# One transformer block with a mixture of experts: the tail of the kernel addressed by token numbers

## The chip, the core and the metric

The kernel runs on one core of one Trainium2 chip. The metric is device time in microseconds (us). Three runs of the kernel before gave 2922.35, 2927.16 and 2928.94 us, a median of 2927.16.

## What is computed

The reference is one adaptive-layernorm block over T = 2048 tokens of width C = 1024, all in float32:

```python
mod = (silu(c) @ wmod)            # six vectors of 1024: sa, ca, ga, sb, cb, gb
h = layernorm(x) * (1 + ca) + sa
x = x + ga * attention(h)         # 32 heads of 32, causal, plus 10 adapter keys, then @ w_proj.T
h = layernorm(x) * (1 + cb) + sb
logits = h @ gate_w               # 8 experts
topv, topi = top_k(logits, 2); w = softmax(topv)
x = x + gb * sum over the two chosen experts e of  w_e * (h @ expert_w[e])     # expert_w[e] is 1024 x 1024
```

Every token is sent to two experts of eight, so there are 4096 pairs of token and expert.

## The kernel before

Every large product is done as three fp32r products: the operands are split into a high half (rounded to fp32r) and a low half (what is left), and hi x hi, hi x lo and lo x hi are added up in PSUM. A split is a copy (the high half) and a subtraction (the low half). SBUF has 128 partitions (P), and C is 8 chunks (KC) of 128. The program is a row of stages; each has its own tiles and semaphores.

- **front** makes the modulation vectors, the layernorm, and q, k and v. In its last part (32 tiles of v, L634 to L641) ScalarE copies each finished PSUM tile out (L280) and the SP queue stores it. Meanwhile the GpSimd (POOL) queue writes zeros over the whole of `scratch_rows`, in 48 DMAs of 512 KB (L521), and in the middle of these it makes two low halves of weights (L488).
- **adapter_attention** and **attention** are not touched.
- **proj_out** (L1348) runs over 16 tiles of 128 tokens in a hardware loop. SP loads the 8 chunks of `w_proj`, then constants, then y and x of the tiles. TensorE waits for all 8 chunks and all constants before its first instruction. For tile n it transposes the normalized rows of tile n - 2 (`turn`, L1407), multiplies tile n (`project`, 48 matmuls at L670 to L672) and makes the 8 logits of tile n - 2 (`gate`, L1414: gate weights stationary, 128 tokens moving). In the first two rounds `turn` and `gate` work on zeros. VectorE scales and adds the residual (L1484, L1486), does the layernorm and hands over to GpSimd (L1516, L1518). x after attention goes to `scratch_x` in HBM, the normalized rows stay in SBUF (`h2`, 64 KB in each partition).
- **route** (L1521) starts when the last tile is done. It finds both experts of all 2048 tokens, the rank of each token within its expert, and from these the row of `scratch_rows` that each of the 4096 pairs gets: the experts' rows follow each other in blocks of 256 rows ("macros"), each expert rounded up to whole macros. Then GpSimd scatters the normalized rows there, 32 indirect DMAs of 512 KB (L1620), and waits until all have landed.
- **experts** (L1625) has an outer loop over the 8 experts and an inner one over the expert's macros; 18 macros in all with these inputs (36 halves of 128 rows, L1778 x36). Weights of the next expert are loaded and split by GpSimd (L1687, L1689) into a second buffer while TensorE works with the first. For each half TensorE turns 128 rows (L1713) and does 48 matmuls; VectorE multiplies by gb (L1778), and the rows go back into `scratch_rows`.
- **combine** (L1781) gathers, for each of 16 tiles, the two rows of each token from `scratch_rows` (32 indirect DMAs, L1799), loads x (L1808), adds the weighted rows (L1824, L1827) and stores the output (L1812).

`scratch_rows` thus links route, experts and combine, and each of them ends with a wait for all of its transfers.

## Time and profile before

| | |
|---|---|
| median of 3 runs | 2927.16 us |
| the profiled execution | 2924.26 us |
| its span, first to last instruction | 2922.4 us |
| TensorE busy | 2508.4 us (86%) |
| VectorE / ScalarE / GpSimd busy | 1422.8 / 903.8 / 1441.1 us |
| DMA | 414.77 MB, mean 142 GB/s |

Busy shares are means over stages that have different limits. The rows of a stretch of time say more: when the last matmul of one stage ends, when the first of the next begins, and what was waited for between them.

### The profile page before, as it was taken

The page shows a single profiled execution, that of the slowest core. Times are in us where ns is not written, and L with a number is a line of the kernel's source. Part 1 is how long each engine was busy: PE and PEld are TensorE (multiplying, and loading weights), DVE is VectorE, ACT ScalarE, POOL GpSimd, SP SyncE. Part 2 cuts the span into 40 slices and gives each one's busy share as a digit, 9 for nine tenths or more (in the row PEclk, how much of TensorE's full clock was granted, in tenths as well). Part 3 has the DMA queues.
Part 4 walks back from the last instruction along what each step waited for, and adds up shares of the span by engine and source line. Part 5 has one row for each costly group of instructions (what it writes and reads, how often), then busy time and mean ns, then how long its engine had stood idle before and what let it go on. Part 6 is the DMA issues. An engine that isn't in the chain of part 4 may idle for free. (4 is left out here: it accounts for less than half of the span.)

```text
span 2922.4 us, 38340 instructions
## 1 busy us (share of the span) xinstructions
PE 2508.4 (86%) x13443; PEld 1624.8 (56%) x13444; DVE 1422.8 (49%) x3025; ACT 903.8 (31%) x1734; POOL 1441.1 (49%) x951
## 2 busy tenths in 40 slices
PE   6789999997759999999999999994999159999970
PEld 4667667775534444444444444442777147878850
DVE  5555455011577777777777777741444122112225
ACT  3511001012314555555555555562111010000000
POOL 4443243022335777777676766772333455465413
PEclk8999999999868999999999999996999579999985
DMA  7355665555453332415152425114564574455339
GB/s 255 102 168 177 183 188 156 209 212 173 174 131 81 81 95 67 117 48 127 42 120 54 114 56 113 38 37 139 179 188 151 201 246 153 138 170 165 115 125 391
DMA packets 222949, 414.77 MB, mean 142 GB/s; under 512 B 31116, under 2 KB 81996, under 8 KB 222676
## 3 DMA queue, kind: packets, MB, share of 16 engines
q1 hardware_dynamic: 182020, 276.54, 33.7%
q0 software_dynamic: 25344, 92.29, 8.8%
q10 hardware_dynamic: 15440, 44.09, 4.0%
q8 instruction: 82, 1.34, 0.2%
q14 instruction: 63, 0.52, 0.1%
HBM read 258.38 MB, written 145.53 MB: 138 GB/s over the span
## 5 line engine op out<-in xcount | busy, mean ns | idle before, releaser
L1315 POOL TENSOR_TENSOR t_two<-t_prob 128x1024 f32<-128x1024 f32 (+1 forms) x321 | 687.2, 2162 | 165.1 <-ACT t_prob L1193 108.2
L1193 ACT ACTIVATE t_prob<-t_scores_psum 128x512 f32<-128x512 f32 (+3 forms) x1280 | 610.9, 537 | 442.6 <-PE t_scores_psum L1085 243.3
L1058 PE MATMUL t_seen_psum<-t_k_stack,t_q_stack 97*128 97x512 f32 (+3 forms) x1283 | 523.3, 420 | 40.0 <-DVE t_q_stack L1209 22.6
L1221 DVE TENSOR_REDUCE t_part<-t_seen_psum 128x1 f32<-128x512 f32 x768 | 479.6, 682 | 143.6 <-PE t_seen_psum L1058 139.5
L1081 PE MATMUL t_scores_psum<-t_q_stack,t_k_stack 98*128 98x512 f32 (+3 forms) x1280 | 503.3, 404 | 5.2 <-ACT t_prob L1193 3.9
L1081 PEld LDWEIGHTS t_scores_psum<-t_q_stack,t_k_stack 98*128 98x128 f32 x1280 | 242.6, 190 | 302.0 <-ACT t_prob L1193 166.1
L1058 PEld LDWEIGHTS t_seen_psum<-t_k_stack,t_q_stack 97*128 97x128 f32 x1283 | 257.3, 201 | 92.9 <-DVE t_part L1221 37.8
L1099 PE MATMUL t_y_acc_psum<-t_prob,t_v 128*32 128x512 f32 (+3 forms) x2576 | 301.3, 540 | 0.0
L1227 DVE CUSTOM_DVE_ANT_0 t_seen_psum<-t_seen_psum,t_causal 128x128 f32<-128x128 f32 (+3 forms) x515 | 250.6, 505 | 100.8 <-PE t_seen_psum L1058 89.6
L670 PE MATMUL e_acc_psum<-e_w_hi,e_x_hi 128*128 128x512 f32 x576 | 231.1, 401 | 0.0
L671 PE MATMUL e_acc_psum<-e_w_lo,e_x_hi 128*128 128x512 f32 x576 | 226.6, 393 | 0.0
L672 PE MATMUL e_acc_psum<-e_w_hi,e_x_lo 128*128 128x512 f32 x576 | 226.5, 393 | 0.0
L611 PE MATMUL f_acc_psum<-hT_hi,f_w_hi 128*128 128x512 f32 x512 | 207.9, 406 | 1.8 <-POOL f_w_lo L473 1.8
L612 PE MATMUL f_acc_psum<-hT_lo,f_w_hi 128*128 128x512 f32 x512 | 202.5, 396 | 0.0
L613 PE MATMUL f_acc_psum<-hT_hi,f_w_lo 128*128 128x512 f32 x512 | 201.9, 394 | 0.0
L483 POOL TENSOR_TENSOR f_y<-f_y,f_y_hi 128x512 fp32r<-128x512 f32 x64 | 83.8, 1309 | 219.9 <-ACT f_y_hi L265 219.5
L1778 DVE TENSOR_TENSOR e_y<-e_acc_psum,e_gb 128x1024 f32<-128x1024 f32 x36 | 44.1, 1225 | 284.4 <-PE e_acc_psum L672 284.4
L1748 ACT ACTIVATE e_x_hi<-e_turned_psum 128x1024 fp32r<-128x1024 f32 x36 | 37.0, 1028 | 411.2 <-DVE e_y L1778 315.8
L1112 PE MATMUL t_total_psum<-t_two,t_ones 128*32 128x512 f32 (+1 forms) x1296 | 155.5, 552 | 1.9 <-POOL t_two L1315 1.9
L265 ACT ACTIVATE f_y_hi<-f_y 128x512 fp32r<-128x512 f32 x64 | 40.4, 632 | 333.7 <-DVEq L412 333.6
L1689 POOL TENSOR_TENSOR e_w_lo<-e_w_raw,e_w_hi 128x1024 fp32r<-128x1024 f32 x56 | 133.7, 2387 | 4.6
L1713 PE MATMUL e_turned_psum<-e_ident,e_x 128*128 128x128 f32 x296 | 46.3, 308 | 97.7 <-DMA e_x<-scratch_rows 67.3
(227 smaller groups left out, 3690.8 us busy)
## 6 DMA issues: line engine op xcount, KB each, us to landing
e_w_raw<-in_expert_w POOLq DMA_DIRECT2D x64, 512.0 KB, 4.4
scratch_rows<-f_y POOLq DMA_DIRECT2D x48, 512.0 KB, 15.0
e_x<-scratch_rows SPq DMA_DIRECT2D x38, 512.0 KB, 4.2
scratch_rows<-e_y ACTq DMA_DIRECT2D x36, 512.0 KB, 4.9
f_w_raw<-in_wmod SPq DMA_DIRECT2D x8, 2048.0 KB, 10.0
t_q_stack<-scratch_q_hi SPq DMA_DIRECT2D x64, 256.0 KB, 5.0
t_k_stack<-scratch_k_hi SPq DMA_DIRECT2D x64, 256.0 KB, 5.1
f_w_raw<-in_w_attn SPq DMA_DIRECT2D x24, 512.0 KB, 7.7
```

What stands on the lines that cost most here:

```text
L611: nc.tensor.matmul(acc[:, n % 2], lhs[0], rhs[0], start=(k == 0), stop=False)
L612: nc.tensor.matmul(acc[:, n % 2], lhs[0], rhs[1], start=False, stop=False)
L670: nc.tensor.matmul(acc, lhs(0, k), rhs(0, k), start=(k == 0), stop=False)
L671: nc.tensor.matmul(acc, lhs(0, k), rhs(1, k), start=False, stop=False)
L672: last = nc.tensor.matmul(acc, lhs(1, k), rhs(0, k), start=False, stop=(k == KC - 1))
L1058: nc.tensor.matmul(seen[:, n % BANKS, 0:width], q_stack[par][0:SEEN, h, t0:t0 + P], k_stack[par][0:SEEN, h, c * CH:c * CH + width], start= ...
L1081: last = nc.tensor.matmul(scores[:, score_bank(step, h), c0:CH], k_stack[par][0:TOPS, h, kt * P:(kt + 1) * P], q_stack[par][0:TOPS, h, qc ...
L1099: last = nc.tensor.matmul(y_acc[h * D:(h + 1) * D, c0:CH], v[par][:, kt, h * D:(h + 1) * D], prob[:, step % RING, h, c0:CH], start=(kt == ...
L1193: nc.scalar.activation(prob[:, step % RING, h, c0:CH], scores[:, score_bank(step, h), c0:CH], ACT.Exp, scale=1.0 / math.sqrt(D)).then_inc( ...
L1221: nc.vector.tensor_reduce(dst, seen[:, n % BANKS], AX.X, ALU.max).then_inc(seen_free, 1)
L1227: nc.vector.tensor_tensor_reduce(out=at, in0=at, in1=causal[:, CH - width:CH], scale=1.0, scalar=MASKED, op0=ALU.add, op1=ALU.max, accum_o ...
L1315: nc.gpsimd.tensor_tensor(two[:, pair % 2, heads, c0:CH], a, b, ALU.add).then_inc(two_ready, 1)
```

## The change

The stages proj_out, route, experts and combine become one stage, `tail`, and the zero fill in front is gone.

- **front:** L513 to L517 and L521, L522 are removed. The two low halves that were made in the middle of them (`even_w`) stay.
- **Projection part:** written out for 16 tiles, without the two rounds on zeros. TensorE starts when y(0) and the 8 constants are there and the first chunk is split, and waits chunk by chunk in tile 0. `gate` has the 128 x 128 activations stationary and the 8 columns of gate weights moving, so the logits come out token by row. x after attention is stored straight into `out`, the normalized rows into `scratch_h2`. In tiles 4 to 11 the weights of expert 0 are split, one chunk in each tile (ScalarE high, VectorE low).
- **Routing:** done in six batches of tiles (4, 4, 3, 3, 1 and 1 tiles), each as soon as its logits are there. What is scattered is no longer a row of 4 KB, but a pair of token number and weight (8 bytes) into `scratch_table`: 32 indirect DMAs of 128 pairs. The table has a fixed region for each expert, filled beforehand with the number 2048, which every gather and scatter skips.
- **Expert loop:** one flat loop over the macros. In every macro SP loads 8 chunks (4 MB) for the next macro, whether or not the expert changes, each as soon as the low half made from its slot is done (eight slots). ScalarE makes the high half of chunk c as soon as the second half of the present macro has used it, VectorE the low half. There is one buffer of split weights. x rows are gathered by token number, two macros ahead. The terms of the experts are added into `out`: gather the rows of `out` (`accin`), `term` = acc x weight x gb, `res` = `term` + `accin`, scatter `res`. GpSimd issues six indirect DMAs in each macro and starts the next gather of `out` only when the scatters have landed.
- **combine** is gone: after the last macro `out` is complete.

The core of the diff, engine by engine (the removed functions are printed above):

In `front`, and the batches of the tail:

```diff
-            for b in range(2):
-                pool.wait_ge(stored[b], 32 * (UNITS // 2))
-            nc.gpsimd.memset(zeros, 0.0).then_inc(zeros_set, 1)
-            pool.wait_ge(zeros_set, 1)
-            for m in range(FILLS * G):
-                if m == FILLS * G // 2:
-                    even_w(5 * HG, 4 * HG + 3)
-                    even_w(5 * HG + 2, 4 * HG + 4)
-                pool.dma_start(rows_d[m * P:(m + 1) * P, :], zeros).then_inc(zeroed, 16)
-            pool.wait_ge(zeroed, 16 * FILLS * G)
+            even_w(5 * HG, 4 * HG + 3)
+            even_w(5 * HG + 2, 4 * HG + 4)
...
+    BATCHES = [(0, 4), (4, 8), (8, 11), (11, 14), (14, 15), (15, 16)]
```

SP, in the expert loop:

```diff
+                def load_chunk(c):
+                    sp.wait_ge(e_lo_done, g * KC + (c + 1))
+                    sp.sem_inc(marks, 1)
+                    src = expert_w[ds(e), c * P:(c + 1) * P, :].rearrange("a p n -> (a p) n")
+                    sp.dma_start(raw_of[c], src).then_inc(w_loaded[c], 16)
+
+                def load_next_ids(s):
+                    sp.wait_ge(x_gathered[s], g * 16 + 32)
+                    sp.sem_inc(marks, 1)
+                    load_ids_x(s, second_after)
+
+                for c in range(5):
+                    load_chunk(c)
+                load_next_ids(0)
+                for c in range(5, KC):
+                    load_chunk(c)
+                sp.wait_ge(acc_free, g * MT + NT)
+                sp.sem_inc(marks, 1)
+                sp.wait_ge(ids_kept, g + 1)
+                sp.sem_inc(marks, 1)
+                sp.dma_start(ids_a[:, :, :], table_d[ds(own, MROWS), :].rearrange("(s p) b -> p s b", p=P)).then_inc(ids_a_loaded, 16)
+                load_next_ids(1)
```

TensorE:

```diff
+            def multiply(g, s):
+
+                pe.wait_ge(x_ready, g * MT + (s + 1))
+                pe.sem_inc(marks, 1)
+                pe.wait_ge(acc_free, g * MT + (NT + s - 1))
                 for k in range(KC):
+                    if s == 0:
+                        pe.sem_inc(marks, 1)
+                        pe.wait_ge(e_lo_done, g * KC + (k + 1))
+                    for o in range(2):
+                        col = slice(o * CH, (o + 1) * CH)
+                        nc.tensor.matmul(acc[:, s, col], x_hi[:, s, k], e_hi[:, k, col], start=(k == 0), stop=False)
+                        nc.tensor.matmul(acc[:, s, col], x_hi[:, s, k], e_lo[:, k, col], start=False, stop=False)
+                        last = nc.tensor.matmul(acc[:, s, col], x_lo[:, s, k], e_hi[:, k, col], start=False, stop=(k == KC - 1))
+                    if s == MT - 1:
+                        last.then_inc(w_used, 1)
...
+            with pe.Fori(0, total) as g:
+                multiply(g, 0)
+                turn_x(g * MT + 2, 0, g * 16 + 32)
+                multiply(g, 1)
+                turn_x(g * MT + 3, 1, g * 16 + 32)
```

ScalarE:

```diff
+                high_x(0, g * MT + (NT + 3))
+                act.sem_inc(marks, 1)
+                for c in range(KC):
+                    act.wait_ge(w_loaded[c], g * 16 + 16)
+                    act.sem_inc(marks, 1)
+                    act.wait_ge(w_used, g * KC + (c + 1))
+                    nc.scalar.activation(e_hi[:, c], raw_of[c], ACT.Copy).then_inc(e_hi_done, 1)
+                high_x(1, g * MT + (NT + 4))
```

VectorE:

```diff
+                def weigh(s):
+                    w = ids_a[:, s, 1:2].bitcast(F32)
+                    nc.vector.scalar_tensor_tensor(out=term[:, s], in0=acc[:, s], scalar=w, in1=gb[:, :],
+                                                   op0=ALU.mult, op1=ALU.mult).then_inc(acc_free, 1)
+
+                def add(s):
+                    dve.wait_ge(gathered[s], g * 16 + 16)
                     dve.sem_inc(marks, 1)
+                    dve.wait_ge(acc_free, g * MT + (NT + s + 1))
+                    nc.vector.tensor_tensor(res[:, s], term[:, s], accin[:, s], ALU.add).then_inc(res_ready, 1)
...
+                dve.wait_ge(acc_ready, g + (NT + 1))
+                dve.sem_inc(marks, 1)
+                dve.wait_ge(ids_a_loaded, g * 16 + 16)
+                dve.sem_inc(marks, 1)
+                dve.wait_ge(res_ready, g * MT + MT)
+                weigh(0)
+                low_x(0, g * MT + 3)
+                for c in range(KC):
+                    low_w(c)
+                dve.wait_ge(w_used, g * KC + KC)
+                weigh(1)
+                add(0)
+                add(1)
+                dve.sem_inc(marks, 1)
+                low_x(1, g * MT + 4)
```

GpSimd:

```diff
+                pool.wait_ge(ids_a_loaded, g * 16 + 16)
+                pool.sem_inc(marks, 1)
                 for s in range(MT):
+                    nc.gpsimd.indirect_dma_start(accin[:, s], None, out, bass.IndirectOffsetOnAxis(ap=ids_a[:, s, 0:1], axis=0),
+                                                 bounds_check=T - 1, oob_is_err=False).then_inc(gathered[s], 16)
+                take_next(0)
+                for s in range(MT):
+                    pool.wait_ge(gathered[s], g * 16 + 16)
                     pool.sem_inc(marks, 1)
+                nc.gpsimd.tensor_copy(ids_y[:, :], ids_a[:, :, 0]).then_inc(ids_kept, 1)
+                pool.wait_ge(ids_kept, g + 2)
+                pool.sem_inc(marks, 1)
                 for s in range(MT):
+                    give(s)
+                take_next(1)
                 for s in range(MT):
+                    pool.wait_ge(scattered[s], g * 16 + 16)
```

## Rows read from the trace of the kernel before

**Rows 1.** Busy time by stretch: PE, PEld, DVE, ACT, POOL, clock, DMA share, GB/s

```profile
2008.00:2033.00 25.00, 1.94 (x8) 1.57 (x8) 9.81 (x8) 10.48 (x10) 1.68 (x1) 0.50 0.92 302
2033.00:2259.00 226.00, 221.25 (x1130) 177.64 (x1131) 85.69 (x181) 22.44 (x45) 72.63 (x30) 0.99 0.55 172
2259.00:2377.00 118.00, 15.72 (x97) 11.98 (x95) 29.24 (x117) 15.20 (x18) 43.06 (x48) 0.55 0.60 223
2377.00:2831.00 454.00, 437.39 (x2013) 363.55 (x2011) 86.98 (x71) 36.99 (x36) 220.56 (x163) 0.97 0.44 142
2831.00:2922.40 91.40, 0.28 (x2) 0.00 (x0) 42.25 (x33) 0.00 (x0) 32.04 (x32) 0.51 0.93 373
```

**Rows 2.** Instructions in time order, v part of front: start, us, engine, [idle before]

```profile
521.04 0.39 PE L634 MATMUL f_acc_psum<-f_w_hi,hT_hi 128*128 128x512 f32 x1
...
526.49 0.39 PE L634 MATMUL f_acc_psum<-f_w_hi,hT_hi 128*128 128x512 f32 x1
...
543.96 0.60 ACT L280 ACTIVATE f_y_hi<-f_acc_psum 128x512 f32<-128x512 f32 x1 [14.64 <-DMA scratch_v<-f_y_hi]
544.61 0.79 PE L634 MATMUL f_acc_psum<-f_w_hi,hT_hi 128*128 128x512 f32 x1 [7.08 <-ACT f_y_hi L280]
...
552.73 0.39 PE L634 MATMUL f_acc_psum<-f_w_hi,hT_hi 128*128 128x512 f32 x1
```

**Rows 3.** Instructions in time order, projection stage, first and last tiles

```profile
2007.72 0.81 SPq L1382 DMA_DIRECT2D o_w_raw<-in_w_proj  x2
...
2047.01 1.23 DVE L1484 TENSOR_TENSOR o_x<-o_acc_psum,o_ga 128x1024 f32<-128x1024 f32 x1 [20.96 <-PE o_acc_psum L672]
...
2258.98 1.23 DVE L1484 TENSOR_TENSOR o_x<-o_acc_psum,o_ga 128x1024 f32<-128x1024 f32 x1 [7.89 <-PE o_acc_psum L672]
...
2268.00 2.34 POOL L1518 TENSOR_TENSOR o_h<-o_h,o_shift 128x1024 f32<-128x1024 f32 x1
```

**Rows 4.** Instructions in time order, routing stage and start of the experts

```profile
2293.05 3.17 DVE L1596 TENSOR_TENSOR r_ahead<-r_count_psum,r_ahead 128x8 f32<-128x8 f32 x16 [0.34 <-PE r_count_psum L1557]
...
2301.32 1.06 POOL L1620 DMA_INDIRECT scratch_rows<-h,slots  x1 [30.98 <-DVEq L1525]
...
2340.35 0.95 POOL L1620 DMA_INDIRECT scratch_rows<-h,slots  x1 [0.30 <-issue]
...
2377.56 0.78 PE L670 MATMUL e_acc_psum<-e_w_hi,e_x_hi 128*128 128x512 f32 x1
```

**Rows 5.** The same view in the expert stage, VectorE's first instruction after each half

```profile
2452.70 1.23 DVE L1778 TENSOR_TENSOR e_y<-e_acc_psum,e_gb 128x1024 f32<-128x1024 f32 x1 [7.49 <-PE e_acc_psum L672]
...
2476.27 1.23 DVE L1778 TENSOR_TENSOR e_y<-e_acc_psum,e_gb 128x1024 f32<-128x1024 f32 x1 [7.50 <-PE e_acc_psum L672]
...
2478.91 1.97 PE L1713 MATMUL e_turned_psum<-e_ident,e_x 128*128 128x128 f32 x8 [2.67 <-issue]
...
2492.55 1.23 DVE L1778 TENSOR_TENSOR e_y<-e_acc_psum,e_gb 128x1024 f32<-128x1024 f32 x1 [9.28 <-PE e_acc_psum L672]
...
2831.32 1.23 DVE L1778 TENSOR_TENSOR e_y<-e_acc_psum,e_gb 128x1024 f32<-128x1024 f32 x1 [7.50 <-PE e_acc_psum L672]
```

**Rows 6.** Groups by line, start of the experts: count, busy us, mean ns, idle before

```profile
L1765 DVE TENSOR_TENSOR e_w_lo<-e_w_raw,e_w_hi 128x1024 fp32r<-128x1024 f32 x8 | 9.8, 1225 | 63.9 <-ACT e_w_hi L1741 63.8
L1741 ACT ACTIVATE e_w_hi<-e_w_raw 128x1024 fp32r<-128x1024 f32 x8 | 8.5, 1057 | 12.2 <-DMA e_w_raw<-in_expert_w 12.2
```

**Rows 7.** GpSimd's gathers in combine: issue ns min/median/max, and us to landing

```profile
L1799 POOL DMA_INDIRECT c_rows<-scratch_rows,slots x32: 932/937/1918, 2836.4 to 2901.4; - x32
...
DMA to landing us min/median/max: 7.3/12.3/14.7
```

**Rows 8.** DMA issues by tile: engine, count, KB each, median us to landing

```profile
scratch_rows<-f_y POOLq DMA_DIRECT2D x48, 512.0 KB, 15.0
...
scratch_rows<-e_y ACTq DMA_DIRECT2D x36, 512.0 KB, 4.9
...
t_inverse<-scratch_inverse SPq DMA_DIRECT2D x132, 64.0 KB, 2.0
```

More of the change, by code:

```diff
@@ new lines, in tail @@
+        indexf, picked = sb("indexf", [P, NT, 8]), sb("picked", [P, 4, E])
+        first, second, both = sb("first", [P, NT, E]), sb("second", [P, NT, E]), sb("both", [P, NT, E])
+        gap, denom, row = sb("gap", [P, NT]), sb("denom", [P, NT]), sb("row", [P, 4, E])
+        ahead, slotf = sb("ahead", [P, NT + 1, E]), sb("slotf", [P, 2, NT])
+        slots, pair = sb("slots", [P, 2, NT], I32), sb("pair", [P, 2, NT, 2], I32)
+        over = spare[0:1, 2 * GN * E:2 * GN * E + E * NTH].rearrange("p (e l) -> p e l", l=NTH)
@@ new lines, in _ @@
+            first_base = at(1)
+            for s in range(MT):
+                sp.wait_ge(x_gathered[s], 16)
+                load_ids_x(s, first_base)
+            sp.wait_ge(e_lo_done, KC)
+            with sp.Fori(0, total) as g:
+                e = sp.value_load(owner_i[0:1, ds(g + 1)], min_val=0, max_val=E - 1)
+                own, second_after = at(g), at(g + 2)
+                def load_chunk(c):
[18 more added lines that the diff above has]
+                load_next_ids(1)
@@ new lines, in _, with turn_x @@
+            for n in range(NT + LAG):
+                if n >= LAG:
+                    turn(n - LAG)
+                if n < NT:
+                    project(n)
+                if n >= LAG:
+                    gate(n - LAG)
+                for b, (n0, n1) in enumerate(BATCHES):
+                    if n == min(n1 + LATE, NT + LAG - 1):
+                        rank(b)
+            def turn_x(m, s, loads):
+                pe.wait_ge(x_gathered[s], loads)
+                if not isinstance(m, int):
+                    pe.sem_inc(marks, 1)
+                if not isinstance(m, int) or m > 0:
+                    pe.wait_ge(x_ready, m)
+                for k in range(KC):
+                    last = nc.tensor.transpose(turned[:, k * P:(k + 1) * P], xt[:, s, k * P:(k + 1) * P], ident[:, :])
+                last.then_inc(turned_ready, 1)
@@ L1872, in adaln_block @@
             attention(nc, sem, consts, (q_hi, q_lo), (k_hi, k_lo), v, a_y, (y_hi, y_lo), scratch("inverse", [HG, CH]))
[L1873 to L1880 removed]
         with semaphores(nc) as sem:
[L1882 to L1883 removed]
+            tail(nc, sem, consts, mod_rows, w_proj, expert_w, (y_hi, y_lo), x, h2, table, out)
 def _constants():
```

786 lines of the change are left out of this document (381 added, 405 removed).

## The prediction

> **What bounds the kernel now.** I read first the busy time by stretch [rows 1], with the stretches cut at the stage boundaries. While a stage multiplies, TensorE is the bound: 221 of 226 us in the projection, 437 of 454 in the expert stage, at a clock of 0.97 to 0.99. Between stages it stands: 25 us at the head of the projection, 118 us between the last projected tile and the first expert matmul, 91 us behind the last matmul. The chain of instructions in time order says why. In the 118 us the chain runs through layernorm, logits and routing, then 32 scatters at 1.26 us each, (2340.35 - 2301.32) / 31, then their landing, the next stage's loads and splits [rows 4]. In the last 91 us nothing but transfers runs, at 373 GB/s [rows 1]. Inside the multiplying stretches two smaller holes matter: 7.08 us in front, where ScalarE waits 14.64 us for stores of v that compete with the zero fill [rows 2], and one at each change of expert [rows 5].
>
> **Part by part. 1, front.** A tile of v takes 5.45 us (521.04 to 526.49). The tile after the hole takes 8.12 us (544.61 to 552.73), since TensorE comes out of the wait at half clock, matmuls of 0.79 us for 0.39. The fills (15.0 us to landing [rows 8]) are what the stores compete with, and they go: 7.1 + 2.7 = 9.7 us. If something else delays the stores, 0. Taking: 9.7.
>
> **2, head of the projection.** The first tile's sum is ready 39.3 us after the stage's first DMA (2047.01 - 2007.72) [rows 3]. TensorE waits there for 8 chunks, 8 constants and y(0), then needs a whole tile. That head moves 302 x 25 = 7.5 MB [rows 1], and the new order needs nearly all of it before the last chunk (2 + 1 + 1.5 + 0.5 + 2 MiB) too, so the last chunk lands at about 25 us. But tile 0 is multiplied chunk by chunk as they land, so behind the last chunk come only a split (1.06 + 1.23 [rows 6]) and six matmuls (1.4): 29 us. That is 10.3 us. Bounds: 0 if the chunks come later, 12 if earlier.
>
> **3, the 16 tiles.** A tile takes 14.13 us ((2258.98 - 2047.01) / 15). 48 matmuls are 10.9 us (twice 5.45), so turn and gate are 3.2 us. One such round less lies between first and last tile (the other is in part 2): 3.3 us. The new work on VectorE (a low half of 1.23 us, or a batch of routing, some 15 small instructions at 3.17 / 16 = 0.2 us [rows 4]) lies in the 5 us and more that it idles in each tile; GpSimd's eight small scatters (10 us) after its 4.7 us of layernorm just exceed one tile, and the normalized rows are wanted 14.13 + 1.9 us after the sum and ready after 11.4 (2258.98 to 2270.34 [rows 3]), so this slack of 4.7 us takes it. Gate with 128 stationary and 8 moving columns I take as equal; half a microsecond each way would be 7 us over 14 tiles. Cost 0. Parts 2 and 3 give 13.6 us (6 to 20).
>
> **4, last tile to first expert matmul.** Before: 2377.56 - 2258.98 = 118.6 us. New, counted from the sum of tile 15: its normalized rows at 11.4 (2270.34 [rows 3]); turn, copy, gate and the first late rank at half clock about 6.5 (17.8). Then VectorE places batch 3 (some 13 small instructions, 2.7), and GpSimd issues 6 + 2 + 2 scatters behind it, 10 x 1.26 = 12.6: 33.2. VectorE's own chain for the last two batches ends at 28.6 and is hidden. Landing of 8-byte pairs 2.5 (35.7), two loads of numbers 2.6 (38.3), of which the row next to it is 2.0 us for a 64 KB load [rows 8]. Gather of x: issue 1.0, landing about 4.9 [rows 8] with a queue that is empty (44.2); turn 1.97 [rows 5], high 1.06, low 1.23 [rows 6], and TensorE turns the second half first, 1.97: 50.4. Gain 118.6 - 50.4 = 68.2 us. If both kinds of indirect DMA land as in combine's full queue, 7.3 to 12.3 [rows 7], it is 60; at 2.0 us each, 73.
> The Trainium skill ("DMA: Bandwidth & Descriptors", on the anatomy of one DMA) gives a transfer 2.0 us plus its bytes over 436 GB/s. For 512 KB that is an estimate of 3.2 us, where the emptier of my rows has 4.9. By it this part would be 1.7 us shorter; no row here has a lone gather.
>
> **5, the expert loop.** TensorE's work in a macro is unchanged: 23.57 us (2452.70 to 2476.27 [rows 5]). A half with a change of expert takes 16.28 (2476.27 to 2492.55) where 11.79 is normal: 2.67 us without work, then half clock. From 2452.70 to 2831.32 there are 30 halves and 6 changes: 378.6 - 30 x 11.79 = 25.0, 4.2 each. The flat loop has none: 7 x 4.2 = 29 us.
> What must fit under 23.57 us, counted from the end of the first half's matmuls. ScalarE: 10 x 1.06 = 10.6. VectorE: 14 instructions of 1.23 = 17.2. GpSimd: 6 x 1.26 = 7.6. Transfers: 8 chunks, two halves of x, two of `out` read, two written, 14 x 0.524 = 7.3 MB, which is 311 GB/s; the trace has 302 to 373 GB/s in full stretches [rows 1], so 19.7 to 24.3 us. Chunk c is freed by TensorE at 0.9 + 1.36 (c + 1), high and low follow at 1.36 us each, the last low half at 14.4, and the next macro's TensorE wants it at 22. VectorE is through at 19.4. Two loops of waits are longest. Numbers: weigh(0) to weigh(1) 14.2 us, then SP loads the next macro's numbers behind 8 chunks, about 4 + 2 us: 20.5. Rows of `out`: add, scatter, landing, gather, landing, two adds: 1.3 + 5 + 2.5 + 7.3 + 2.5 = 18.6. Both fit. The PE's extra counts and waits (nine in a macro) are in its queue and I take them as 0. So 424.7 us instead of 453.7. At the worst transfer rate it is 0.7 x 18 = 13 us more.
>
> **6, the end.** Before: 2922.4 - 2831.3 = 91.1 us. New: the last high and low half of the weights nobody uses 2.6, weigh 1.3, two adds 2.5, scatter issued 1.1, landing 5, the last gather and the end of the program 2: 14.5. Gain 76.6 us (70 to 80).
>
> **Sum.** 9.7 + 13.6 + 68.2 + 29.0 + 76.6 = 197.1 us. The profiled execution took 2924.26 us (its span 2922.4 and 1.9 around it), so 2727; it lay 2.9 below the median of 2927.16, so 2730.
>
> **Rivals.** *The expert loop is bound by transfers and their landings.* For it: 311 GB/s against 142 now, and a loop of waits at 20.5 of 23.6 us; combine's gathers land after 12.3 us at 373 GB/s [rows 7]. [...] Against: transfers are spread, and weights are wanted 20 us after they are asked for. A macro of 26 to 30 us gives 18 x 2.4 to 6.4 = 44 to 116 us: 2774 to 2846.
> The Trainium skill ("SBUF — State Buffer", on the two separate sides) says that VectorE and GpSimd share one pair of ports, which a VectorE instruction with two SBUF inputs holds only against a GpSimd one that reads SBUF, and in a fast mode also against the writing of descriptors. All low halves on VectorE would then not hold up GpSimd's DMAs. The longest issue in combine is 1.92 us against 0.93 [rows 7], beside instructions of VectorE; six such would lengthen the loop through `out` by some 4 us, still under 23.6.
> *TensorE drains at every count and wait between the chunks.* Nothing in the trace has this form in the middle of matmuls. The nearest price is 2.67 us for a change of expert, which holds several register loads and a wait for TensorE's own end; a ninth of it each, 0.3, over 9 places and 18 macros is 49 us: 2779.
> *Slower than before.* The loop through `out` is serial: scatter, landing, gather, landing. If each landing were over about 14 us, as GpSimd's DMAs were in front (15.0 [rows 8]) and combine's at most (14.7 [rows 7]), a macro would take 6.3 + 2 x 14.1 = 34.5 us, 10.9 over, and 18 x 10.9 = 197 us eat the whole gain. At 15 to 17 us each, 2960 to 3035. Against it: those landings had 24 or 8 transfers of 512 KB queued at once, here two or three.
> *The change does not do what it says:* the holes stay because the stage waits for something else at its seams (stores of h, clearing `xt`, the tables). These end before 38 us in part 4; if not, 10 to 20 us more, within the range.
>
> **Chances.** Forecast (2710 to 2755) 0.58; transfers bind 0.26; draining 0.08; slower 0.05; no change at all under 0.01; better than 2710 the rest. The range takes the first and most of the second and third: 2712 to 2820. A measurement of this kernel tells 0.2%, 6 us, from no change. Faster 0.94, same 0.01, slower 0.05.
>
> **What would show it.** Right: no hole near 540 us; first expert matmul some 50 us behind tile 15's sum; 23.6 us between VectorE's first weighings of two macros, with TensorE's share over 95% there; 14 us behind the last matmul. Wrong: TensorE waiting for a low half of weights (transfers, or ScalarE and VectorE one behind the other), for x rows, or gaps of 0.2 us and more at each chunk; gathers of `out` that end VectorE's idle time; landings above 10 us. The likeliest mistake is in the two loops of waits of part 5, where every microsecond counts eighteen times.

## The result, and the profile after

The changed kernel takes 2750.77 us, the median of 4 runs (2747.71 to 2751.94), against 2926.77 us (4 runs, 2922.35 to 2928.94) for the kernel before: a ratio of 0.9399, with a 95% interval of 0.9383 to 0.9415. The prediction was 2730 us (2712 to 2820). The profiled execution took 2750.97 us; its span is 2748.7 us.

First the busy time by stretch, cut where the parts of the prediction end: head of the projection, its 16 tiles, the way to the first expert matmul, the expert loop, the end. Columns as in [rows 1].

```profile
1997.40:2027.60 30.20, 13.02 (x50) 10.64 (x51) 10.08 (x12) 9.74 (x9) 0.62 (x4) 0.66 0.93 306
2027.60:2244.90 217.30, 205.51 (x1073) 175.91 (x1072) 124.79 (x275) 34.39 (x59) 97.28 (x46) 0.97 0.71 194
2244.90:2302.80 57.90, 16.72 (x74) 15.02 (x72) 25.68 (x100) 5.59 (x11) 23.10 (x21) 0.50 0.16 50
2302.80:2727.40 424.60, 424.60 (x2009) 354.19 (x2009) 297.83 (x248) 186.95 (x179) 123.87 (x124) 1.00 0.82 291
2727.40:2748.70 21.30, 1.04 (x9) 0.80 (x7) 6.99 (x6) 1.97 (x2) 3.17 (x3) 0.60 0.12 48
```

TensorE is busy in all of the 424.60 us of the loop, at full clock. In the kernel before, the expert stage had it busy 437 of 454 us [rows 1]. Elsewhere the new stage fell short of the forecast, in three places. The first is in the projection, where TensorE works 205.51 of 217.30 us (instructions in time order, as [rows 3]):

```profile
2027.59 1.23 DVE L1706 TENSOR_TENSOR z_x<-z_acc_psum,z_ga 128x1024 f32<-128x1024 f32 x1 [4.48 <-PE z_acc_psum L1544]
...
2176.09 0.81 DVE L1724 TENSOR_SCALAR z_h<-z_x,z_mv,z_rstd 128x1024 f32<-128x1024 f32 x1 [7.76 <-DMA scratch_h<-z_h]
...
2183.58 0.69 PE L1521 MATMUL z_turned_psum<-z_ident,z_h 128*128 128x128 f32 x2 [7.40 <-POOL z_h L1862]
...
2238.22 0.82 DVE L1724 TENSOR_SCALAR z_h<-z_x,z_mv,z_rstd 128x1024 f32<-128x1024 f32 x1 [7.33 <-DMA scratch_h<-z_h]
...
2243.93 1.97 PE L1521 MATMUL z_turned_psum<-z_ident,z_h 128*128 128x128 f32 x8 [3.10 <-POOL z_h L1862]
...
2244.87 1.23 DVE L1706 TENSOR_TENSOR z_x<-z_acc_psum,z_ga 128x1024 f32<-128x1024 f32 x1
```

Twice VectorE may not overwrite the normalized rows, because their store of two tiles earlier has not landed. GpSimd then starts late, and TensorE stands for 7.40 and 3.10 us before its turn; each time it comes back at half clock (1.97 us for a turn that takes 1.07 in the tiles between). The landing times of the two kinds of transfer that meet there, the stores (L1634) and the scatters of pairs (L1871):

```profile
L1634 ACTq DMA_DIRECT2D scratch_h<-z_h x16: 333/444/6084, 2043.3 to 2256.7; - x16
...
DMA to landing us min/median/max: 2.6/6.7/24.7
```

```profile
L1871 POOL DMA_INDIRECT scratch_table<-z_pair,z_slots x32: 952/958/1512, 2145.5 to 2278.5; - x32
...
DMA to landing us min/median/max: 5.0/11.2/20.6
```

The issue of one of the stores also kept ScalarE's queue for 6.08 us, where the median is 0.44; in e1, below, none takes over 0.45.

The second place is the chain on the way to the experts (start, duration, what it went through):

```profile
2278.46 10.97 DMA scratch_table<-z_pair,z_slots
2289.43 0.02 issue
2289.45 1.70 DMA z_ids_x<-scratch_table
```

The last scatter of 1 KB lands after 10.97 us, where the prediction has 2.5. The third is at the end, the drains, the instructions with which the engines leave the stage:

```profile
L1348 DVEq DRAIN  x1: 3030/3030/3030, 2731.5 to 2731.5; - x1
L1348 POOLq DRAIN  x1: 9211/9211/9211, 2738.4 to 2738.4; - x1
```

At 2738.4 all rows have landed; GpSimd then drains for 9.21 us, and nothing moves any more.

Part by part, in us (what is worked out is a difference of two starts in the profiled executions; the first line is the time at which the stage starts, the others are durations):

| part | before | predicted | after | missing |
|---|---|---|---|---|
| 1: start of the stage | 2007.7 | 1998.0 | 1997.4 | -0.6 |
| 2 and 3: start to tile 15's sum | 251.3 | 237.7 | 247.5 | 9.8 |
| 4: to the first expert matmul | 118.6 | 50.4 | 57.9 | 7.5 |
| 5: the expert matmuls | 453.7 | 424.7 | 424.6 | -0.1 |
| 6: behind them | 91.1 | 14.5 | 21.3 | 6.8 |
| sum of the gains | | 197.1 | 173.7 | 23.4 |

The stages between front and tail, which are the same in both kernels, differ from one execution to the next: from front's last matmuls to the start of the tail they take 1315.5 to 1324.0 us in the eleven profiled executions of kernels with the new tail (before: 1320.9). So one execution's total says little below 5 us. The parts of the tail repeat better, and the experiments are read from them and from the medians.

### The profile page after: what moved, and what is told of

It is laid out like the page before. It is cut to its first block and busy times, and to the rows that moved or that the text cites. A ratio compares the mean times of both kernels' runs of the same rounds, so it can differ in the third digit from the quotient of the medians.

```text
span 2748.7 us, 40013 instructions
## 1 busy us (share of the span) xinstructions
PE 2491.0 (91%) x13407; PEld 1625.9 (59%) x13407; DVE 1631.2 (59%) x3253; ACT 1056.0 (38%) x1885; POOL 1292.5 (47%) x827
## 5 line engine op out<-in xcount | busy, mean ns | idle before, releaser
L1306 POOL TENSOR_TENSOR t_two<-t_prob 128x1024 f32<-128x1024 f32 (+1 forms) x321 | 687.2, 2163 | 168.7 <-ACT t_prob L1184 105.5
L1591 PE MATMUL z_acc_psum<-z_e_hi,z_x_hi 128*128 128x512 f32 x576 | 228.0, 396 | 0.0
L1593 PE MATMUL z_acc_psum<-z_e_hi,z_x_lo 128*128 128x512 f32 x576 | 224.9, 390 | 0.0
L1592 PE MATMUL z_acc_psum<-z_e_lo,z_x_hi 128*128 128x512 f32 x576 | 224.5, 390 | 0.0
L1542 PE MATMUL z_acc_psum<-z_p_hi,z_y_hi 128*128 128x512 f32 x256 | 102.6, 401 | 34.1 <-DMA z_gate_w<-in_gate_w 34.1
L1665 ACT ACTIVATE z_x_hi<-z_turned_psum 128x1024 fp32r<-128x1024 f32 x38 | 38.7, 1018 | 223.0 <-PE z_turned_psum L1577 223.0
L602 PEld LDWEIGHTS f_acc_psum<-hT_hi,f_w_hi 128*128 128x128 f32 x512 | 98.2, 192 | 41.1 <-issue 10.3
L1593 PEld LDWEIGHTS z_acc_psum<-z_e_hi,z_x_lo 128*128 128x128 f32 x576 | 108.4, 188 | 23.1
## 6 DMA issues: line engine op xcount, KB each, us to landing
f_w_raw<-in_wmod SPq DMA_DIRECT2D x8, 2048.0 KB, 10.5
```

Of the source, the lines that this page charges most:

```text
L602: nc.tensor.matmul(acc[:, n % 2], lhs[0], rhs[0], start=(k == 0), stop=False)
L1306: nc.gpsimd.tensor_tensor(two[:, pair % 2, heads, c0:CH], a, b, ALU.add).then_inc(two_ready, 1)
L1591: nc.tensor.matmul(acc[:, s, col], x_hi[:, s, k], e_hi[:, k, col], start=(k == 0), stop=False)
L1592: nc.tensor.matmul(acc[:, s, col], x_hi[:, s, k], e_lo[:, k, col], start=False, stop=False)
L1593: last = nc.tensor.matmul(acc[:, s, col], x_lo[:, s, k], e_hi[:, k, col], start=False, stop=(k == KC - 1))
```

## The experiments

### Are the scatters the cause of the waits in the projection? (e1, e2)

`e1_sends_last` issues all scatters behind the last tile, `e2_sends_spread` two or four a tile:

```diff
 for n in range(NT):
     scale(n)
-    for b, (n0, n1) in enumerate(BATCHES[:-3]):
-        if n == n1 + LATE + 1:
-            send(b)
-for b in range(len(BATCHES) - 3, len(BATCHES)):
+for b in range(len(BATCHES)):
     send(b)
```

> All 32 scatters of pairs go behind the last tile's layernorm. Theory A (GpSimd's 8-byte scatters make the stores of the normalized rows land late, VectorE waits 7.8 and 7.3 us for them, and TensorE then stands 7.4 and 3.1 us and restarts at half clock): in the projection no wait of VectorE for a store above 2 us, first to last tile sum about 208 us instead of 217.3, no TensorE hole above 1 us there. Theory B (the stores are late of their own, behind ScalarE's issues and the other loads): both holes stay where they are. In both, the stretch from the last tile's sum to the first expert matmul grows: 32 scatters at 1.26 us are issued in a row behind 2256.4, the last one at about 2296, 18 us later than now, and the landing behind it is 10 to 15 us; so 57.9 becomes 74 to 85 us. Total by A 2757 to 2766 us, by B 2766 to 2777.

> The scatters of the first eight tiles go out two or four in a tile instead of eight at once in two tiles; what follows the last tile is unchanged (the six scatters of tiles 8 to 10 first). Theory A (backlog: 8 scatters of 128 pairs occupy the transfer engines for some 22 us, and the stores issued meanwhile wait for them): with two in a tile the backlog is about 6 us, VectorE's wait for the store of the rows of two tiles earlier falls from 7.8 and 7.3 us to under 1 us, TensorE's holes of 7.4 and 3.1 us go, and the projection is 8 to 10 us shorter: 2741 to 2744 us. Theory B (any scatter beside the loads of a tile delays the stores by its whole landing of 11 us): the waits become smaller but more numerous, and the total stays within 3 us of 2751.

e1: 2752.07 us, ratio 0.941 (0.9392 to 0.9427), below what either theory had. The stretch from its first to its last sum (columns as in [rows 1]), and the stores in it:

```profile
2027.50:2228.30 200.80, 200.00 (x1055) 171.19 (x1053) 126.56 (x274) 34.31 (x59) 80.03 (x30) 1.00 0.61 207
```

```profile
L1634 ACTq DMA_DIRECT2D scratch_h<-z_h x16: 333/444/445, 2043.2 to 2240.1; - x16
...
DMA to landing us min/median/max: 2.6/5.6/9.5
```

That is 200.8 us instead of 217.3 (theory A had 208), with no wait for a store; TensorE is busy for 200.00 of these 200.80 us, and the slowest store lands after 9.5 us instead of 24.7. To the experts it takes 75.6 us instead of 57.9. What one part gained the other lost. That the scatters delay the stores is shown: without them beside the tiles both waits are gone.

The same run says how a scatter lands with nothing beside it: each of the 32 goes out 1.26 us behind the one before, the first lands after 6.8 us, all others after 9.5 to 12.4. From 2250 us on nothing else moves (1 GB/s), and they don't get slower and slower: this is no queue that grows, and no competition with loads.

e2: 2743.48 us, 0.9388 (0.9369 to 0.9407). From the first to the last sum 206.6 us; three waits for a store are left, 9.9 us in all, the longest, 7.4 us, behind the tile with four scatters. The scatters' median landing is still 10.2 us. So spreading shortens the projection, though the total can't be told from the changed kernel's (0.9388 and 0.9399, with intervals that overlap). My backlog of some 22 us, which was to shrink with the burst, is not the mechanism: in a later run (e9) two scatters a tile were enough for a store that landed after 22.4 us.

### What makes a scatter of 8-byte pairs slow? (e7, e10)

Two programs of their own, which leave the block out and only copy x to the output; GpSimd issues sets of 8 scatters of 128 rows.

> A program of its own that leaves the whole block out and copies x to the output: GpSimd issues 8 indirect scatters of 128 rows, six times, each set alone: rows of 8 bytes next to each other; rows of 8 bytes, 128 apart; rows of 64 bytes; of 512 bytes; of 4 KB; and last again rows of 8 bytes, beside 12 loads of 512 KB on SP's queue and stores of 512 KB on ScalarE's. Theory A (a small row costs the transfer engines the same whatever its size: 1.6 us for 128 of them when little else runs, 3.2 beside loads): the first four sets are alike, the eighth scatter lands some 8 us after its issue, and the 4 KB rows are limited by bytes (512 KB at 373 GB/s, 1.4 us). Theory B (rows under 512 bytes are written more slowly, by a read and a write): the 512-byte rows land in half the time of the 64- and 8-byte rows or less. In the last set the eighth scatter lands after 15 to 20 us, as in the changed kernel, and ScalarE's stores after 10 us or more instead of 4 to 6.

```profile
scratch_near<-data,idx_near POOLq DMA_INDIRECT x8, 3.3
scratch_far<-data,idx_far POOLq DMA_INDIRECT x8, 2.1
scratch_row4k<-data,idx_near POOLq DMA_INDIRECT x8, 4.2
scratch_busy<-data,idx_near POOLq DMA_INDIRECT x8, 10.3
```

The last number of a row is the median landing in us. Both theories fail. Rows of 8 bytes 128 bytes apart land after 2.1 us, rows of 64 and 512 bytes after 2.1 and 2.2 us, so neither the number of rows nor their size is slow, with only neighbouring rows a little slower (3.3). The last set, beside loads and stores, lands after 10.3 us, under the 15 to 20 expected, and the stores beside it after 6.4 (median), not 10 or more. None of the quiet sets comes near the 10 us of e1. What it did not have was e1's order: in the kernel the pairs of one expert stand next to each other, and come from tokens (partitions) all over the tile.

> A program of its own again (it leaves the block out and copies x to the output). The first probe's scatters landed after 2.1 us (3.3 to 3.9 where the 8-byte rows of one transfer were neighbours, 10.3 beside loads), while in the kernel with all scatters behind the projection each lands after 9.5 to 12.4 us though nothing else runs. What differs is the order of rows: there, neighbouring rows come from partitions far apart. Six sets of 8 scatters: neighbouring 8-byte rows in a transposed order (partition p to row 16 (p mod 8) + p/8); rows as random routing to 8 experts gives them, 8 bytes each; the same with rows of 64 bytes; of 512 bytes; and again 8 bytes and 64 bytes beside 6 loads and 2 stores of 512 KB each. Theory A (writes of different transfer engines into the same 64 bytes wait for one another): the first two sets land after 7 to 11 us, those with rows of 64 and 512 bytes after 2 to 3 us; beside loads 15 us or more against 10 or less. Theory B (the landing in the kernel has another cause, such as the size of the table or what the queue did before): all four quiet sets land after 2 to 4 us.

```profile
scratch_turned<-data,idx_turned POOLq DMA_INDIRECT x8, 3.2
scratch_small<-data,idx_routed POOLq DMA_INDIRECT x8, 9.2
scratch_mid<-data,idx_routed POOLq DMA_INDIRECT x8, 2.1
scratch_wide<-data,idx_routed POOLq DMA_INDIRECT x8, 2.2
scratch_smallbusy<-data,idx_routed POOLq DMA_INDIRECT x8, 18.2
scratch_midbusy<-data,idx_routed POOLq DMA_INDIRECT x8, 5.4
```

With rows in routed order, 8 bytes apart, the landing is 9.2 us (5.1 for the first, up to 11.1); with the same order and rows of 64 bytes it is 2.1, and 512 bytes add nothing to that. Beside loads and stores it is 18.2 against 5.4. So theory A holds in its core: what is slow is small records close to one another, in this order. How close is known only roughly: 8 bytes apart is slow, 64 isn't, and nothing between was tried, so "the same 64 bytes" of the theory is not shown. Its first set failed (3.2 us in the transposed order, not 7 to 11): it is not enough that neighbours of one transfer come from other partitions. Nor is it enough that several transfers at a time write close together: in the first probe's `scratch_far` scatter j writes row 16 p + j from partition p, so for each p all eight write into the same 64 bytes, two of them under way at a time, and they land after 2.1 us. The routed order has both, neighbours from other partitions and from the next transfer. Whether it is the two together, or the random order, I did not separate.

The Trainium skill ("DMA: Bandwidth & Descriptors", Specifications) says that below 512 bytes the transfer engines read, modify and write. By it alone 64-byte rows would be slower than 512-byte ones; here they are 2.1 and 2.2 us, and the trace disagrees with it as a price. Whether it is how close writes come to wait for each other, no run here shows.

### The remedy in the kernel (e11)

`e11_wide_rows` writes the same 8 bytes at every 64th:

```diff
-table = nc.dram_tensor("scratch_table", [TABLE, 2], I32).ap()
+table = nc.dram_tensor("scratch_table", [TABLE, 16], I32).ap()
...
-r.link(nc.vector.tensor_copy(slots[:, :, at], slotf[:, :, at]))
+r.link(nc.vector.tensor_scalar(slots[:, :, at], slotf[:, :, at], float(PITCH // 2), None, ALU.mult))
...
-nc.gpsimd.indirect_dma_start(table_d, bass.IndirectOffsetOnAxis(ap=slots[:, c, i:i + 1], axis=0),
+nc.gpsimd.indirect_dma_start(table_d.rearrange("t (k b) -> (t k) b", b=2), bass.IndirectOffsetOnAxis(ap=slots[:, c, i:i + 1], axis=0),
```

> The changed kernel with the rows of the table 64 bytes apart instead of 8 (the same 8 bytes are written and read; the table is filled with 1.1 MB instead of 137 KB). Theory A (neighbouring 8-byte rows written by different engines hold one another up, and this backlog delays the stores): scatters land after 2 to 4 us when nothing else runs, 11 us less 3 is 8 us off the stretch from the last tile's sum to the first expert matmul (57.9 to 50), and in the projection VectorE no longer waits for the stores of the normalized rows: 217.3 to 202 us. Total 2751 - 8 - 15 = 2728 us (2724 to 2734). Theory B (a small write costs this much wherever it lands): landing 10 to 11 us as before, holes stay, 2748 to 2754 us.

2725.78 us (2717.75 to 2729.12), ratio 0.9303 (0.9284 to 0.9322). The chain behind the last scatter, to be laid beside that of the changed kernel:

```profile
2262.86 2.10 DMA scratch_table<-z_pair,z_slots
2264.96 0.02 issue
2264.97 1.76 DMA z_ids_x<-scratch_table
```

10.97 us became 2.10. First to last sum 200.8 us with the scatters in their old places, none of them delaying a store for which VectorE waits; last sum to first expert matmul 49.1. Both are the numbers of theory A, and the ratio is 1.0 points (28 us) better than the changed kernel's. This settles the missing time of parts 3 and 4: it went with the distance between the pairs, whatever makes close ones slow.

### How near is the expert loop to its limit? (e4, e4b)

Two more chunks of weights in every macro, into tiles that nobody reads; in `e4b_numbers_act` the numbers of the present macro come over ScalarE's queue:

```diff
 for c in range(5):
     load_chunk(c)
+    if c < EXTRA:
+        load_extra(c)
...
-sp.dma_start(ids_a[:, :, :], table_d[ds(own, MROWS), :].rearrange("(s p) b -> p s b", p=P)).then_inc(ids_a_loaded, 16)
+act.dma_start(ids_a[:, :, :], table_d[ds(own, MROWS), :].rearrange("(s p) b -> p s b", p=P)).then_inc(ids_a_loaded, 16)
```

> In every macro of the expert loop SP loads two more chunks of weights (512 KB each) into tiles that nobody reads any more: 16 x 0.524 = 8.39 MB in a macro instead of 7.34. Theory A (the loop is bound by TensorE, and the transfers have slack up to some 373 GB/s, the mean of the old last stage): 356 GB/s, a macro still takes 23.58 us and the total stays within 3 us of 2751. Theory B (the transfers only just keep up at 311 GB/s; the landing times grow first, of weights 5.5 us and of the rows 4.5 us): a macro takes 8.39 MB / 311 = 27.0 us, 3.4 x 18 = 61 us more, 2812.

> As the run with two extra chunks of weights in each macro (loop 461.7 us, 25.65 a macro), but the 2 KB load of token numbers and weights of the present macro goes over ScalarE's queue instead of SP's, where it stood behind the 512 KB loads and landed after 11.8 us (4.3 in the changed kernel). Theory A (the extra loads cost time only because the numbers land behind them, VectorE's first weighing waits, and with it the split of x and TensorE's turn): the numbers land in 5 us or less, VectorE's waits for them go, a macro takes 23.6 to 23.9 us again and the total is 2748 to 2757 us. Theory B (313 GB/s is what this mix of transfers can do at most): the macro stays at 25.6 us and the total at 2794.

e4: 2794.39 us, 0.955 (0.9535 to 0.9565), the loop 461.7 us, 25.65 a macro. VectorE's wait for the numbers between 2350 and 2700 us (who, for what, us in all, times, longest) and the busy time of the same stretch, first of e4 and then, with the numbers moved, of e4b:

```profile
DVE z_x_in L1843 <- DMA z_ids_a<-scratch_table: 140.1, 14, 11.5
```

```profile
2350.00:2700.00 350.00, 327.28 (x1513) 265.40 (x1512) 220.14 (x193) 140.91 (x135) 108.30 (x95) 1.00 0.83 308
```

```profile
DVE z_x_in L1844 <- DMA z_ids_a<-scratch_table: 44.5, 7, 7.1
```

```profile
2350.00:2700.00 350.00, 350.00 (x1665) 292.06 (x1664) 247.47 (x208) 153.88 (x148) 110.39 (x105) 1.00 0.91 338
```

In e4 no wait for a weight stands at the top of the list. VectorE waits in nearly every macro for 2 KB of numbers, which land after 11.8 us behind the 512 KB loads in the same queue. Both my figures missed (23.58 and 27.0 us a macro). With that one load on another queue (e4b) the extra weights cost nothing: 2751.09 us, 0.941 (0.9391 to 0.9429), loop 424.7 us, TensorE busy 350.00 of 350 us with 338 GB/s moving. The numbers still land after 7.6 us, not the 5 or less of theory A, and VectorE waits for them seven times; no matmul is lost by it. So the loop of the changed kernel is not bound by transfers, and has room for at least two chunks more; what it has little room in is the loop of the numbers.

How little shows in the runs whose loop has the same code as the changed kernel, with the last two for comparison. The landing of that load (min, median, max), what VectorE waits for it between 2350 and 2700 us (in all, times), and the 18 macros:

| run | landing of the numbers | VectorE's wait for them | expert matmuls |
|---|---|---|---|
| e3 | 3.7 / 4.1 / 9.0 | none | 424.9 |
| e1 | 3.7 / 4.2 / 8.7 | none | 424.7 |
| e11 | 3.8 / 4.2 / 9.0 | none | 425.5 |
| changed kernel | 3.7 / 4.3 / 8.5 | none | 424.6 |
| e6 | 5.6 / 6.6 / 10.0 | 79.6, 11 | 424.3 |
| e2 | 5.6 / 7.2 / 10.2 | 117.5, 15 | 428.3 |
| e12 | 5.7 / 7.9 / 10.5 | 105.5, 14 | 429.5 |
| e9 (other order on GpSimd) | 6.0 / 8.7 / 10.3 | 131.4, 14 | 448.1 |
| e4 (two more chunks) | 9.3 / 11.8 / 13.1 | 140.1, 14 | 461.7 |

In the changed kernel 8.4 us lie between the load's issue and VectorE's next weighing, which there still waits for TensorE:

```profile
2495.63 0.38 SPq L1498 DMA_DIRECT2D z_ids_a<-scratch_table  x1
...
2504.00 1.28 DVE L1824 SCALAR_TENSOR_TENSOR z_x_in<-z_acc_psum,z_ids_a,z_gb 128x1024 f32<-128x1024 f32 x1 [5.27 <-PE z_acc_psum L1593]
```

In e6 VectorE waits for the numbers, and TensorE loses nothing by it; from a median of 7.2 us on the loop is longer. The same code settles in one rhythm (4.1 to 4.3 us) or another (6.6 to 7.9), and I do not know what chooses.

### The first stage (e3)

`e3_fills_back` puts the removed lines back into front, into a scratch that nobody reads.

> The 48 DMAs of zeros (512 KB each) are put back into the first stage, into a scratch that nobody reads. Theory A (the fills delay the stores of v; ScalarE, then TensorE, wait): the hole of about 7 us near 540 us returns, and the matmuls behind it run at half clock; the last matmul of the stage ends some 10 us later, and the whole is 2761 us (2758 to 2763). Theory B (the hole was there for another reason, such as the split of weights on GpSimd between the fills): it does not return, 2751 us.

2761.88 us (2750.76 to 2770.42), ratio 0.9453 (0.9433 to 0.9474), 0.5 points or 16 us over the changed kernel, give or take 8. The two rows to be laid beside [rows 2]:

```profile
541.91 0.60 ACT L279 ACTIVATE f_y_hi<-f_acc_psum 128x512 f32<-128x512 f32 x1 [14.74 <-DMA scratch_v<-f_y_hi]
...
542.56 0.80 PE L633 MATMUL f_acc_psum<-f_w_hi,hT_hi 128*128 128x512 f32 x1 [7.04 <-ACT f_y_hi L279]
```

14.64 and 7.08 us there, 14.74 and 7.04 here: the fills make the hole. Front's last matmuls start at 683.99 us, in ten profiles without fills at 672.8 to 678.5, a mean of 675.7. So the fills cost 8.3 us there; the rest of the 16 I can't place. The profiled execution doesn't help: at 2750.76 us it is the fastest of the four, with the shortest way of all from front to tail (1315.5 us).

### The end (e6)

Three multiplications on GpSimd (7.17 us) behind its loop.

> Behind the loop GpSimd does three multiplications of 128 x 1024 whose result nobody uses (7 us in all), before the end of the program. In the changed kernel the last 9.2 us are GpSimd's drain, with no transfer in them; it ends 10.7 us after GpSimd's last DMA was issued. Theory A (the drain lasts until some 10.7 us after the last DMA issue, whatever GpSimd does meanwhile): the three multiplications are hidden in it, the drain is about 2 to 3 us, the stretch behind the last matmul stays at 21.3 us. Theory B (the drain takes its 9.2 us after whatever came last): 21.3 + 7 = 28.3 us, total 7 us more.

2758.18 us, 0.944 (0.9422 to 0.9458). Behind the last matmul 28.8 us instead of 21.3, and GpSimd's drain is 9.21 us again. Theory A is out: the drain does not run from the last DMA issue but takes its time after whatever comes last. It is 9.21 us in all eleven profiles of the new tail and 9.16 us at the end of the adapter stage of the changed kernel, 16.3 us in the last stage of the kernel before, where transfers covered it, and 0.05 us in the changed front (3.99 with the fills in it, before and in e3). What sets it stays open.

### Putting it together (e9, e12, e13)

`e9_combined` keeps the table at 8 bytes a row.

> The changed kernel with four edits: batches of 3, 3, 3, 2, 3, 1, 1 tiles; the scatters of the first 11 tiles at two a tile (four in two of them) as soon as they are ready; TensorE makes the ranks of tiles 11 to 13 before the last gate instead of behind it; GpSimd's last gather of x is issued ahead of the two scatters of out. Theory A (the backlog of small scatters is what the projection and the transition lost): first to last tile sum 201 to 204 us (217.3 in the changed kernel), last tile to first expert matmul 47 to 50 us (57.9), since the last scatter is issued some 8 us earlier and lands after 5 to 7 us instead of 11, behind the last matmul 20.0 (21.3): 2751 - 15 - 9 - 1.3 = 2726 us (2722 to 2732). Theory B (the landing of the last small scatter is 10 us whatever is queued before it; ranks and the layernorm set the end): the transition stays above 54 us, 2732 to 2740 us.

2764.2 us, 0.9459 (0.9433 to 0.9485), slower than the changed kernel, where both theories had it faster. The projection had two waits for a store, 8.25 and 4.01 us (first to last sum 211.6), the way to the experts fell to 52.4, and the loop grew to 448.1 us. Its new order,

```diff
+take_next(1)
 for s in range(MT):
     give(s)
-take_next(1)
```

sends for 512 KB of x while the load of the numbers is under way, and that load lands after 8.7 us. That this order is the cause is an argument: no run has the order alone. e13 has it again, with the numbers on another queue.

> The table with rows 64 bytes apart, and two edits of order: TensorE makes the ranks of tiles 11 to 13 before its last gate instead of behind it, and GpSimd issues the scatters of tiles 8 to 10 behind the layernorm of tile 14 instead of that of tile 15. Theory A (with quick landings the stretch behind the last tile is set by GpSimd's 16 scatters in a row, and by when VectorE has the last rows): the last scatter is issued some 28 us behind the last tile's sum instead of 33.6, and the stretch to the first expert matmul shrinks from 49.1 to 43 to 46 us: 2719 to 2724 us. Theory B (the tables of macros and the clearing of the x tile on VectorE come behind, and set the end): the stretch stays above 48 us, 2725 us.

> The same kernel, with GpSimd's last gather of x issued ahead of the two scatters of out, and the load of the present macro's numbers on ScalarE's queue. The first of these edits stood in the combined kernel whose expert loop took 448.1 us, with VectorE waiting for the numbers in every macro (landing 8.7 us, against 4.3 in the changed kernel). Theory A (the numbers were late there because they stood behind weights in SP's queue and beside GpSimd's transfers): over ScalarE's queue and asked for earlier, they are there in time, the loop is 424.5 to 426 us, the stretch behind the last matmul 20.0 instead of 21.3, since GpSimd's last DMA is issued 1.3 us earlier; 1 us better than the kernel beside it, 2718 to 2723 us. Theory B (asking for the rows of x before the scatters of out lengthens the loop of out itself, whoever loads the numbers): the loop stays at 440 to 448 us and the total at 2735 to 2745.

The order on TensorE and on GpSimd, in both kernels:

```diff
+if n == NT + LAG - 1:
+    rank(len(BATCHES) - 3)
 if n >= LAG:
     gate(n - LAG)
...
-    if n == n1 + LATE + 1:
+    if n == min(n1 + LATE + 1, NT - 2):
         send(b)
```

e12: 2722.51 us, 0.9292 (0.9273 to 0.9311). Last sum to first expert matmul 44.8 us, as theory A has it, but the loop took 429.5. e13: 2719.64 us (2717.38 to 2722.19), 0.9295 (0.9279 to 0.9312), with 44.9 us and a loop of 424.3: over ScalarE's queue the numbers land after 1.8 us, and with them there GpSimd's order does no harm, so e9's 448.1 us were not the loop of `out`. The end is 22.7 us, not 20.0, a miss: the gather in front of them puts the last scatter 8.6 us behind the last matmul instead of 7.2, and with it its landing, after which the drain of 9.21 us begins. The intervals of e11, e12 and e13 overlap. All three are below both kernels, by 28 to 31 us against the changed one.

## Why the prediction was right, and what was off

**Part 1** held: front's last matmuls start 9.3 us earlier (686.80 and 677.48) for 9.7, TensorE no longer waits for ScalarE there, and e3 brings the hole back in both its numbers. The 10.3 us at the start of the tail hold 1.0 us of the stages between, which is chance.

**Part 2**: 30.2 us for 29. TensorE multiplies as the chunks come; 306 GB/s were moving at the head, 302 before [rows 1].

**Part 3** took the new scatters as costing GpSimd's time alone ("this slack of 4.7 us takes it"). That step failed. The slack was there for the layernorm, but the stores of the same rows had none against the scatters: two waits of 7.8 and 7.3 us, and with the half clock behind them 217.3 - 200.8 = 16.5 us (e1, e11). The loss seems smaller because the tiles were otherwise shorter than I had them: 200.8 us for the 15 from first to last sum (e1), where mine were 15 x 14.13 - 3.3 = 208.7. A full tile takes 13.53 us. The gate itself is equal, as taken: 1.84 us for 16 pieces, 1.91 before. Among what went is a wait of the gate for ScalarE's copy, 0.56 us in the tile at 2131.73 of the kernel before, which I did not list. That these 8 us stood against 16.5 of loss, and brought the total nearer to the forecast, is luck.

**Part 4** had every step on its path, and one was mis-sized: "landing of 8-byte pairs 2.5" was 10.97 us, 8.5 more. It is the number with the least behind it in the prediction; the rows next to it were a plain 64 KB load and gathers of 4 KB rows. With rows 64 bytes apart 2.5 would have been right (2.10), and the part comes out at 49.1 for 50.4. The gather of x landed after 4.4 us for 4.9. The bound of 60 us of gain took 7.3 us for both landings; with 12.3, the other end of its row, it would have been 51, and with 2.0 it is 72 and not 73. The measured gain, 60.7, meets the 60 by chance: one landing was longer and the other shorter than 7.3.

**Part 5** held to 0.1 us. A macro takes 23.58 us (2338.94 to 2362.52 between VectorE's first weighings), the counts and waits on TensorE cost nothing, and the change of expert is gone. I took 7.3 MB for a macro; 291 GB/s in the loop is 6.9 MB. The kernel skips rows past an expert's last pair, 4608 - 4096 = 512 of 4 KB in each of three transfers, which is 0.35 MB a macro. Of the two loops named as near their limit, that of `out` has 11.2 us to spare (GpSimd's wait for VectorE's rows, 2485.97 to 2497.36), that of the numbers 4 us by its median landing (8.4 - 4.3). The first I had at 18.6 of 23.6 us, and it is 12.4.

**Part 6** took 2 us for the last gather and the end of the program. That term was mis-sized. Up to the landing of the last rows it took 11.0 us (2727.4 to 2738.4), where the sum has 12.5; behind it came 10.3 us, of which GpSimd's drain, 9.21 us, was in no term. In the kernel before it stood beside transfers, where it cost nothing.

**The rivals.** *Transfers bind* was wrong in its mechanism at this load: TensorE waits for nothing in the loop, and with two chunks more and the numbers out of the way it still doesn't, at 338 GB/s. But its "loop of waits at 20.5 of 23.6 us" is that of the numbers, which comes first, as e4, e9 and e12 show. *Draining* had no sign: TensorE is busy in all 424.60 us of the 36 halves. *Slower than before* (the serial loop through `out`) needed landings over 14 us; gathers landed after 4.5 us and scatters after 3.5 (medians). *The change does not do what it says* named the stores of h at the seams; there they held up nothing, but inside the projection they did (part 3). By the Trainium skill ("SBUF — State Buffer", on the two separate sides) low halves on VectorE, which have two inputs from SBUF, don't hold up the writing of descriptors for GpSimd's DMAs. In the loop its three kinds of indirect DMA take 1.00 to 1.06 us to issue (medians; 5 of 106 take over 1.2, the longest 1.98), and the trace agrees.

The profiled execution came out 24 us above its forecast of 2727: 8.5 from the landing of the pairs, 6.8 from the end, 16.5 from the waits for stores, less some 8 for shorter tiles.

## What to carry to other kernels

Before small records are scattered, look at who writes their neighbours: 8 bytes at a pitch of 64 cost a larger table, took the landing from 11 us to 2 and ended the delay of the stores in another queue. Where a loop stands well under its bandwidth, the small load that everything waits for is the one to watch: ask what is queued ahead of it, and give it a queue of its own before weights are blamed. And when covering work is removed from the end of a program, list what it covered, each engine's last instructions too.

## What the runs showed of the hardware

- Scatters of 128 records of 8 bytes in routed order land after 9.2 us (median, 5.1 to 11.1) with nothing beside them, and after 18.2 us beside loads and stores; records of 64 bytes in the same order after 2.1 and 5.4 us (e10). In the kernel, 8 bytes written 64 bytes apart land after 2.10 us, the last scatter of e11. Between 64-byte and 512-byte records there is next to no difference (2.1 and 2.2 us).
- Where such scatters meet other transfers, the transfer engines can be booked full and move little. The changed kernel's rows for a stretch without scatters, the one in which the first eight go out, and the one behind it (columns as in [rows 1]):

```profile
2040.00:2060.00 20.00, 20.00 (x103) 16.98 (x102) 9.96 (x23) 2.56 (x5) 6.97 (x3) 1.00 1.03 358
2140.00:2160.00 20.00, 20.00 (x104) 17.01 (x102) 7.77 (x18) 2.48 (x5) 17.51 (x12) 1.00 0.73 146
2160.00:2180.00 20.00, 15.70 (x90) 13.58 (x89) 11.15 (x29) 5.01 (x7) 4.97 (x2) 0.97 1.07 160
```

  A DMA share of 1.07 goes with 160 GB/s in the last row, one of 1.03 with 358 GB/s in the first. Stores issued then landed after up to 24.7 us. With nothing beside them the scatters book next to nothing: the share is 0.02 in e1, from 2250 to 2290 us.
- A load of 2 KB behind 512 KB loads in the same queue landed after 4.3 us (median), and after 11.8 with two chunks more in a macro (e4); on ScalarE's queue, with none of those loads ahead of it, after 1.8 us (e13), or 7.6 with the two chunks more (e4b).
- GpSimd's drain at the end of the tail took 9.21 us, whether DMAs or 7.17 us of arithmetic (e6) stood before it.
